# A macaron block on one core: a second norm moved to GpSimd, loads split and moved, orders of five queues rewritten

## The reference

```python
def ffn(x):                       # weights of -1, 0, 1; scales s per output
    h = silu(x @ w1.T * s1) * (x @ w2.T * s2)    # 128 -> 512
    h = gelu(h @ h1.T * sh1)                     # 512 -> 512
    h = gelu(h @ h2.T * sh2)                     # 512 -> 512
    return h @ w3.T * s3                         # 512 -> 128
def att(x):
    h = layernorm(x) * gamma + beta
    k, v = h @ Wk.T + bk, h @ Wv.T + bv
    e = exp((k @ Wka.T + bka) / sqrt(128))
    e = e / cumsum(e, axis=1)
    return cumsum(e * k, axis=1) * v
x = x + 0.5 * ffn(layernorm(x))
x = x + att(x)
x = x + 0.5 * ffn(layernorm(x))
```

## Time and profile before

| | |
|---|---|
| Median of 3 runs | 368.09 us (367.99 to 369.10) |
| The profiled execution | 368.15 us, its span 366.4 us |
| Instructions | 5194, of them 1578 products and 251 on GpSimd |
| Busy | TensorE 98%, VectorE 86%, ScalarE 77%, GpSimd 45% |
| Chain of waits | TensorE 96%, VectorE 2%, ScalarE 1%, issue 1% |
| Loads and stores | 20.94 MB, 57 GB/s on the mean |

### The profile page before, as it was taken

How to read it: one execution, slowest core, us unless ns; L and a number is a source line. 1 busy time by engine, 2 the same in 40 slices (tenths; PEclk the granted TensorE clock), 3 DMA queues, 4 the chain that set the end, 5 groups by cost and what they waited for, 6 DMA issues and landing times.

```text
span 366.4 us, 5194 instructions
## 1 busy us (share of the span) xinstructions
PE 359.3 (98%) x1578; PEld 285.1 (78%) x1578; DVE 316.2 (86%) x550; ACT 283.1 (77%) x465; POOL 163.3 (45%) x251
## 2 busy tenths in 40 slices
PE   7999999999999999999999999999999999999996
PEld 2678888787877777788778787787778777888885
DVE  5999688999989998889899989998899799857642
ACT  4998777987777879776887968877897697686763
POOL 3553344649045565812685545652573740530000
PEclk9999999999999999999999999999999999999999
DMA  7770103030100301300222012012022020040001
GB/s 245 270 294 4 54 3 107 8 110 9 58 2 0 86 29 36 83 0 2 59 59 59 1 59 59 0 59 86 0 59 88 2 86 2 4 111 2 1 30 63
DMA packets 16256, 20.94 MB, mean 57 GB/s; under 512 B 7008, under 2 KB 8288, under 8 KB 15968
## 3 DMA queue, kind: packets, MB, share of 16 engines
q1 hardware_dynamic: 15504, 19.75, 18.2%
q10 hardware_dynamic: 720, 0.80, 0.7%
HBM read 18.36 MB, written 2.18 MB: 56 GB/s over the span
## 4 chain that ended last, share of the span: by engine, by line
PE 96%; DVE 2%; issue 1%; ACT 1%; POOL 0%; POOLq 0%; ACTq 0%
PE hid_ps L643 62%; PE gate_ps L643 8%; PE y_ps L643 8%; PE up_ps L643 7%; PE y_ps L662 2%; PE xt_ps L829 2%; PE xt_ps L833 2%; PE xt_ps L836 2%; PE y_ps L843 1%; PE gate_ps L707 1%; PE up_ps L707 1%; DVE gate L1070 0%; PE xt_ps L643 0%; DVE xt_sb L1142 0%; PE xt_ps L656 0%
## 5 line engine op out<-in xcount | busy, mean ns | idle before, releaser
L643 PE MATMUL hid_ps<-act_hi,hi_h 128*128 128x512 f32 x480 | 193.3, 403 | 0.0
L643 PE MATMUL hid_ps<-act_lo,hi_h 128*128 128x512 f32 x480 | 186.7, 389 | 0.0
L1092 DVE TENSOR_TENSOR act_lo<-full,act_hi 128x512 fp32r<-128x512 f32 x185 | 132.8, 742 | 23.6 <-ACT act_hi L909 20.6
L902 ACT ACTIVATE full<-hid_ps,vec 128x512 f32<-128x512 f32 x123 | 84.1, 687 | 57.2 <-PE hid_ps L643 51.7
L643 PEld LDWEIGHTS hid_ps<-act_hi,hi_h 128*128 128x128 f32 x480 | 90.3, 188 | 22.8 <-issue 2.6
L643 PEld LDWEIGHTS hid_ps<-act_lo,hi_h 128*128 128x128 f32 x480 | 90.2, 188 | 21.3 <-issue 2.6
L909 ACT ACTIVATE act_hi<-full 128x512 fp32r<-128x512 f32 x127 | 78.6, 628 | 1.6
L567 POOL TENSOR_TENSOR xnt<-xt_sb,wide 128x512 f32<-128x512 f32 x21 | 29.4, 1400 | 45.8 <-DMA wide<-rows 45.8
L885 ACT ACTIVATE tanh<-gate_ps,s_half 128x512 f32<-128x512 f32 x60 | 40.4, 680 | 7.4 <-PE gate_ps L643 7.3
L1070 DVE SCALAR_TENSOR_TENSOR gate<-tanh,gate_ps 128x512 f32<-128x512 f32 x60 | 40.3, 674 | 6.5 <-ACT tanh L885 6.4
L1082 DVE SCALAR_TENSOR_TENSOR full<-up_ps,s_half,gate 128x512 f32<-128x512 f32 x60 | 44.1, 741 | 1.1
(11 more groups left out here) (170 smaller groups left out, 440.3 us busy)
## 6 DMA issues: line engine op xcount, KB each, us to landing
wide<-rows SPq DMA_DIRECT2D x42, 256.0 KB, 3.7
xt_sb<-xt SPq DMA_DIRECT2D x1, 2048.0 KB, 10.6
out<-xt_sb SPq DMA_DIRECT2D x7, 256.0 KB, 4.0
x_sb<-x SPq DMA_DIRECT2D x1, 1536.0 KB, 6.8
raw_h<-h2t SPq DMA_DIRECT2D x4, 256.0 KB, 7.1
raw_h<-h1t SPq DMA_DIRECT2D x2, 256.0 KB, 6.1
rows<-pair SPq DMA_DIRECT2D x21, 4.0 KB, 2.2
raw_w<-w2t ACTq DMA_DIRECT2D x1, 256.0 KB, 4.0
```

The source lines that it names most:

```text
L643: mm = eng.matmul(ps, w, a, start=(first and n == 0), stop=(last and n == len(seq_) - 1))
L902: eng.activation(full23[m % 2][:, :], home23(n, T, m)[:, :], ACT.Gelu, scale=col("sh1" if n == 2 else "sh2", m)).then_inc(s_gelu[n], 1)
L1092: eng.tensor_tensor(act_lo[a][:, m, :], full[m % 2][:, :], act_hi[a][:, m, :].bitcast(F32), ALU.subtract).then_inc(s_lo[n], 1)
```

## The change

It does these things together:

- The ones products go from 4 + 2 + 1 to 4 + 1, and the wait for the first power between them goes too.
- Tile 2 leaves `BY_PE`: its norm goes by GpSimd, the parked rows and the wide reads, as those of tiles 3 to 7. Norms aggregated on GpSimd count from 2 instead of 3.
- Act 1 of odd tiles lies in the second pair of buffers, that of even tiles in the first; before, only tile 1 used the second.
- SyncE loads x of tiles 2 and 3, and xt of tile 2, of tiles 0 and 1, and of tile 3, each by itself. x and xt of tiles 4 to 7 (1 MB each) are issued by ScalarE, just ahead of `high2.0` of tile 0.
- GpSimd's rounding of h2 and w3 becomes part of its order: h2 chunk 0 ahead of tile 2's norm, the other three and w3 behind it.
- In tile 0's first layer the half products stand in another order, flag sum 2 stands behind p1.3 in another bank (`gate_ps` instead of `y_ps`) and p1.3 no longer waits for it; `norm` of tile 0 is split into three entries.
- The orders of all five queues are written anew, the second layer of tile 0 too.

The diff, cut to its core:

```diff
-WARM_UP = (4, 2, 1)
+WARM_UP = (4, 1)
 START = {
     "PE": (
         "flag:sum1 t",
-        "p1.0 p1.1 flag:sum2 p1.2 p1.3",
+        "p1.0 p1.1 p1.2 p1.3 flag:sum2",
     ),
     "ACT": (
         "hi:w1 hi:w2 z",
-        "t vec:s1 bits:h1.1 bits:h1.3 tanh.0 tanh.1 tanh.2 high1.0 tanh.3 high1.1 z.0 z.1 high1.2 bits:h2.0 "
-        "high1.3 1:t",
+        "t vec:s1 tanh.0 bits:h1.1 bits:h1.3 bits:h2.0",
     ),
     "DVE": (
-        "stats aggr veps bits:w1 bits:w2 norm",
-        "flag:copy1 bits:h1.0 t vec:scales bits:h1.2 stats flag:raise2 aggr gate.0 veps flag:copy2 up.0 gate.1 "
-        "up.1 low1.0 gate.2 up.2 gate.3 up.3 bits:h2.1 low1.3 1:t",
+        "stats aggr veps bits:w1 bits:w2 norm.0 norm.1 norm.2 flag:copy1 0:t bits:h1.0 vec:scales bits:h1.2",
+        "gate.0 stats flag:raise2 up.0 aggr gate.1 flag:copy2 veps up.1 low1.0 gate.2 up.2 gate.3 up.3 "
+        "bits:h2.1 bits:h2.2 low1.3 1:t 2:stats flag:raise3 flag:copy3 1:gate.0 0:low2.0 1:up.0 0:low2.1 "
+        "1:gate.1 1:up.1 0:low2.2 0:low2.3 1:low1.0 1:gate.2 1:low1.1 1:gate.3 1:up.2 1:up.3",
     ),
 }
 SECOND_LAYER = (
-    "p2ahi.0 p2ahi.1 p2ahi.2 p2ahi.3 p2alo.1 p2alo.3 p2bhi.3 p2alo.0 p2alo.2 p2bhi.0 p2bhi.2 t p2blo.0 p2bhi.1 "
-    "p2blo.1 p2blo.3 p2chi.0 p2blo.2 p2clo.0 p2dhi.0 p2chi.1 p2chi.2 p2clo.1 p2dlo.0 p2chi.3 p2dhi.1 p2clo.3 "
-    "p2clo.2 p2dlo.1 flag:sum3 p1.0 p2dhi.2 p2dhi.3 p1.1 p2dlo.2 p2dlo.3"
+    "p2ahi.0 p2ahi.2 p2ahi.1 p2ahi.3 p2alo.3 p2alo.0 p2bhi.0 p2alo.2 p2alo.1 p2blo.0 p2blo.1 t p2bhi.3 "
+    "p2chi.2 p2blo.3 p2chi.0 p2chi.1 p2chi.3 p2bhi.1 p2clo.2 p2blo.2 p2dhi.2 p2clo.0 p2dhi.0 p2dlo.0 p1.0 "
+    "p2clo.1 flag:sum3 p2dhi.1 p2dlo.1 p2bhi.2 p2clo.3 p1.1 p2dlo.2 p2dhi.3 p2dlo.3"
 )
...
     "POOL": (
-        "norm",
+        "hi:h2.0 norm hi:h2.1 hi:h2.2 hi:h2.3 hi:w3 xn.0 xn.1",
         "norm xn.0 xn.1",
...
     "PE": (
-        "p1.2 p1.3 fold p3.0 p3.1",
-        "t 0:p3.2 p1.0 0:p3.3 p2.0 p1.1 p2.1 p2.2 p2.3 p4 p1.2 p1.3 a0:u p3.0 p3.1 p3.2 p3.3",
+        "p1.2 p1.3 p3.0 p3.1 p3.2 fold p3.3",
+        "p1.0 p1.1 p2.0 p2.1 p1.2 p4 p2.2 a0:u p2.3 p1.3 p3.0 p3.1 p3.2",
...
     "ACT": (
-        "bits:w3 bits:h2.3 gelu2.0 high2.0 gelu2.1 tanh.0 high2.1 tanh.1 gelu2.2 gelu2.3 high2.2 high1.0 "
-        "high2.3 high1.1 tanh.2 z gelu3.0 tanh.3 2:t high3.0 gelu3.1 high1.2 high3.1 gelu3.2 high1.3 high3.2 "
-        "gelu3.3 high3.3",
+        "0:tanh.1 0:tanh.2 0:high1.0 0:tanh.3 0:high1.1 1:z.0 1:z.1 0:high1.2 bits:w3 t 0:high1.3 bits:h2.3 "
+        "gelu2.0 tanh.0 high2.0 gelu2.1 high2.1 tanh.1 gelu2.2 gelu2.3 tanh.2 high2.2 high2.3 high1.0 high1.1 "
+        "tanh.3 gelu3.0 gelu3.1 high3.0 high3.1 high1.2 2:t high1.3 gelu3.2 high3.2 2:tanh.0 gelu3.3 high3.3",
...
     "DVE": (
-        "bits:h2.2 flag:raise3 stats low2.0 flag:copy3 aggr gate.0 veps low2.1 gate.1 up.0 up.1 low2.2 low2.3 "
-        "fold low1.0 gate.2 3:stats up.2 low1.1 2:t gate.3 up.3 low3.0 low1.2 low3.1 low1.3 low3.2 low3.3",
+        "3:stats 2:t low3.0 low3.1 low1.2 low1.3",
...
-BY_PE = (0, 1, 2)
-AGGREGATE = 3
+BY_PE = (0, 1)
+AGGREGATE = 2
...
         def first_act(T):
-            return "second" if T == 1 else 1
+            return "second" if T % 2 else 1
...
-            xload(2, NT, s_xr)
+            xload(2, 3, s_x2t)
+            eng.dma_start(xt_tile(2), xt[:, 2 * TOK:3 * TOK]).then_inc(s_xt2, 16)
+            xload(3, 4, s_x3t)
...
-            eng.dma_start(xt_sb[:, :], xt).then_inc(s_xt, 16)
+            eng.dma_start(xt_sb[:, 0:2 * TOK], xt[:, 0:2 * TOK]).then_inc(s_xt, 16)
+            eng.dma_start(xt_tile(3), xt[:, 3 * TOK:4 * TOK]).then_inc(s_xt3, 16)
...
-                    for h in range(2):
-                        for part_of, ready, first in ((xn_hi, s_xhi_half, True), (xn_lo, s_xlo_half, False)):
+                    for h, low, up in ((0, 0, 0), (0, 0, 1), (0, 1, 0), (1, 0, 0), (0, 1, 1), (1, 1, 0), (1, 0, 1), (1, 1, 1)):
...
             warm_up(WARM_UP[0])
             eng.wait_ge(s_ve, 1)
             warm_up(WARM_UP[1])
-            eng.wait_ge(s_pow, 1)
-            warm_up(WARM_UP[2])
...
             def high23(n, T, m):
+                if (n, T, m) == (2, 0, 0):
+                    eng.wait_ge(s_w3, 16)
+                    eng.dma_start(x_sb[:, 4 * TOK:], x[:, 4 * TOK:]).then_inc(s_xr, 16)
+                    eng.dma_start(xt_sb[:, 4 * TOK:], xt[:, 4 * TOK:]).then_inc(s_xtr, 16)
```

More of the change, by code:

```diff
@@ L51 @@
     "SP": (
-        "",
+        "park wide",
         "park wide",
         "a0:park a0:wide park wide",
-        "a1:park park a1:wide wide",
+        "a1:park a1:wide park wide",
         "park wide",
@@ L62 @@
         "park wide",
-        "a6:park 8:store a6:wide park wide",
-        "a7:park a7:wide 9:store park wide",
-        "10:store park 11:store wide store",
+        "a6:park a6:wide park wide",
+        "a7:park 8:store 9:store a7:wide park wide",
+        "park 10:store 11:store store wide",
         "store",
@@ L387, in items @@
                     yield stage, chunk, int(which) if which else i + AHEAD.get(stage, 0)
-        norm_of = {("ffn", t): t for t in range(2)}
-        for i, order in enumerate(STEPS["DVE"]):
+        norm_of = {}
+        for i, order in enumerate(START["DVE"] + STEPS["DVE"], -2):
             for stage, _, t in items(order, i):
@@ L428, in flag_home @@
         def flag_home(part):
-            return (hid_ps[0], y_ps, xt_ps)[part - 1][0:1, 0:1]
+            return (hid_ps[0], gate_ps[0], xt_ps)[part - 1][0:1, 0:1]
         def turn_home(n):
@@ L602, in _ @@
                     low1(stage)
-            for k in range(MC):
-                hi("h2", k)
-            hi("w3", 0)
             def emit(stage, chunk, t):
-                if stage in ("norm", "att_norm"):
+                if stage == "hi":
+                    hi(t, chunk or 0)
+                elif stage in ("norm", "att_norm"):
                     kind = "ffn" if stage == "norm" else "att"
@@ L670, in p1 @@
                         eng.wait_ge(s_whi[n], 1)
-                    for h in range(2):
-                        for part_of, ready, first in ((xn_hi, s_xhi_half, True), (xn_lo, s_xlo_half, False)):
-                            eng.wait_ge(ready, h + 1)
-                            for ps, n, done in ((gate_ps[0], "w1", s_gp), (up_ps[0], "w2", s_p1)):
-                                moved = halves(part_of, h)
-                                w, moved = (raw, moved.bitcast(F32)) if general else (whi, moved)
-                                mm = eng.matmul(halves(ps, h), wblk(w, n, 0, 0), moved, start=first, stop=not first)
-                                if not first and h == 1:
-                                    mm.then_inc(done, 1)
+                    for h, low, up in ((0, 0, 0), (0, 0, 1), (0, 1, 0), (1, 0, 0), (0, 1, 1), (1, 1, 0), (1, 0, 1), (1, 1, 1)):
+                        ready, moved = (s_xlo_half, xn_lo) if low else (s_xhi_half, xn_hi)
+                        eng.wait_ge(ready, h + 1)
+                        ps, n = (up_ps[0], "w2") if up else (gate_ps[0], "w1")
+                        moved = halves(moved, h)
+                        w, moved = (raw, moved.bitcast(F32)) if general else (whi, moved)
+                        mm = eng.matmul(halves(ps, h), wblk(w, n, 0, 0), moved, start=not low, stop=bool(low))
+                        if low and h == 1:
+                            mm.then_inc(s_p1 if up else s_gp, 1)
                     return
-                if (T, m) in ((0, 3), (1, 1)):
-                    eng.wait_ge(s_flag, T + 2)
+                if (T, m) == (1, 1):
+                    eng.wait_ge(s_flag, 3)
                 if T == 1:
@@ L1055, in norm_veps, with first_norm @@
                 eng.tensor_scalar(veps[:, :], mv[:, :, 1], 1.0, EPS, ALU.mult, ALU.add).then_inc(s_ve, 1)
[L1057 removed]
+            def first_norm(j):
                 eng.wait_ge(s_pow, 1)
[L1060 to L1062 removed]
+                eng.tensor_scalar(z[:, j * P:(j + 1) * P], norm_blk("ffn", 0, j), mv[:, j, 0:1], rstd[:, j:j + 1],
+                                  ALU.subtract, ALU.mult).then_inc(s_z, 1)
             def gate(T, m):
@@ L1117, in emit @@
                 elif stage == "norm":
-                    first_norm()
+                    first_norm(chunk)
                 elif stage == "t" and t == 0:
```

34 lines of the change are left out of this document (16 added, 18 removed), and 169 rows, old and new, of the table STEPS.

## The result

The changed kernel takes 372.85 us (median of 4 runs, 371.52 to 373.44), the kernel before beside it 368.17 (367.99 to 369.10). The ratio is 1.0117, 95% interval 1.0099 to 1.0135: slower by 1.2%, and outside the predicted range.

The account below looks back on a forecast made before the run. TensorE, busy 98% of the span, was taken to bound the kernel. From 368.15 us, gelu2.3 +0.15, turns -0.45, fold -0.07 and the wait for tile 2 +1.3 gave +0.9, so 369.0; range 367.0 to 370.2.

Parts of the forecast that it names:

- the hold: Tile 2's norm: the park waits amid ScalarE's loads, landing at 28.0, so TensorE waits 1.3 us for xn_lo.
- Turns and fold: TensorE at tile 2: four turns fewer save 0.45 us, a product's start-up saved at the fold 0.07.
- The likeliest case: Tile 2's rows are held behind ScalarE's loads: 369.0 us, between 368.4 and 369.8; chance 42%.
- rival T: Follow-up forecast for 2 KB pieces: queues alternate piece by piece, park landed near 27.5, 369 to 370 us; no chance given.
- case D: At the start, two fewer ones products let TensorE idle and delay the 2.4 GHz step: +2, 370.1 us; chance 9%.
- The start: Up to p1.3 of tile 1: first-turn gain given back, 0; gelu2.3 later behind two load issues, +0.15 us.
- the hand walk: Instruction times laid out over the first 36 us: tanh 0 at 9.35, gate 1 at 12.6, second layer from 14.1.
- ScalarE's two issues: Two loads issued ahead of high2.0 delay gelu2.3, which p1.3 waits for, by 0.15 us; bounds 0 and 0.9.
- Case C: First turn's gain is kept, tile 0's second layer starts and ends 0.5 us earlier: 366.8 us; chance 17%.

Follow-up runs that it names:

- run 1: Changed kernel with ScalarE's two 1 MB loads issued later, ahead of high3.0 instead of high2.0: 368.73 us, ratio 1.0011.
- run 9: Kernel before with ones products 4 + 1 and no wait for the first power, nothing else of the change: 368.38 us, ratio 0.9991.
- run 6: Changed kernel with ScalarE's two loads issued at the same place as four of 512 KB, in pieces of 2 KB: 371.35 us, ratio 1.0071.
- run 4: Changed kernel with five ones products put ahead of tile 2's first product to fill TensorE's pause: 371.35 us, ratio 1.0088.
- loads on SyncE (8): Changed kernel with the two 1 MB loads issued by SyncE behind xt of tile 3, instead of by ScalarE: 369.21 us, ratio 1.0030.
- run 11: The version of run 10 with ones products 4 + 1 at the start instead of 4 + 2 + 1: 367.89 us, ratio 0.9991.
- both edits (3): Changed kernel with ones products 4 + 2 + 1 again and ScalarE's loads ahead of high3.0: 368.16 us, ratio 0.9998.
- run 10: Version with both edits (3), plus three ones products behind flag sum 2 in the pause before the second layer: 367.92 us, ratio 0.9986.
- run 12: The same kernel as run 10, measured once more: 368.66 us, ratio 1.0004.
- run 2: Changed kernel with the ones products as before, 4 + 2 + 1, and the wait for the first power: 374.17 us, ratio 1.0147.
- run 7: Changed kernel with load x left ahead of high2.0 and load xt moved ahead of high3.0: 368.43 us, ratio 0.9998.
- run 5: Changed kernel with loads written for 2 KB pieces, which stayed at 8 KB, so a repeat of the changed kernel: 373.59 us, ratio 1.0131.

## Why the prediction was wrong

The start of p1.3 of tile 1 splits the 4.97 us by which the profiled span grew.

| | before | changed | predicted | measured |
|---|---|---|---|---|
| p1.3 of tile 1 starts | 25.50 | 26.76 | +0.15 | +1.26 |
| from there to the end, without the hold | 340.87 | 340.15 to 340.40 | -0.52 | -0.47 to -0.72 |
| waits for tile 2's xn_hi and xn_lo | 0 | 2.09 + 0.41 | +1.3 | +2.50 |
| clock at the 1.2 GHz level | 0 | 38.66 to 42.08 | 0 | +1.57 |
| rest | | | 0 | +0.11 to 0.36 |

The second line is the span less the start of p1.3 in the six profiles with neither a wait at tile 2 nor a fall behind it: 340.15 (run 1), 340.22 (8), 340.29 (3), 340.33, 340.37 and 340.40 (10 to 12). The fourth is the difference between profiles of the same work, with and without the fall: the thirteenth product behind the first that reads xn_lo comes 4.66 us after it in the changed kernel (38.23 to 42.89), 3.09 in its repeat (38.32 to 41.41) and 3.08 in the filled one (37.13 to 40.21). The spans agree: less p1.3's start and the two waits, the changed kernel has 371.34 - 26.76 - 2.50 = 342.08 and its repeat 369.73 - 26.58 - 2.73 = 340.42, beside the 340.15 to 340.40 of the six.

**Turns and fold: right.** The one term called a sure gain is there in all six; the two profiles of the old order have 340.87 and, run 9, 366.38 - 25.01 = 341.37. That these two differ by 0.5 with the same work bounds what such a comparison can tell.

**The hold: right in kind, too small: the term that was mis-sized.** The likeliest case put the park at 28.0 behind ScalarE's loads, because two queues took turns packet by packet. The place and the culprit hold (run 1), and so do the turns. What the working left out is that the park's pieces may come to the engines late: 3.5 to 3.6 us behind the issue in the five profiles with all of ScalarE's loads ahead of it, 0.9 to 1.0 with none or one (runs 1 and 7). With pieces of 8 KB the landing is the loads' end either way, since some ten of them an engine were left at 25.4, one microsecond behind the park's issue; with 2 KB (run 6) turns from the start would by the estimate of rival T have landed the park near 27.5, and it landed near 30.5. The term was mis-sized by the loads' end: issued at 21.68 instead of 21.1, and landed at 30.45 instead of 27.9, 8.4 us after the second issue, where 6.8 from a 1.5 MB load was used for 2 MB. With it the park landed 2.7 later than forecast (30.67), xn_lo was done at 38.2 instead of 35.8, while TensorE came 1.16 later itself: 1.3 + 2.4 - 1.16 = 2.5.

The rule of the Trainium skill, "DMA: Bandwidth & Descriptors", "Queues, rings and completion order", that an engine changes queue after some 9 to 17 descriptors, is contradicted by run 6: between 29.44 and 30.44 us one engine changed queue after every single piece.

**The clock: the step that failed outright.** The prediction weighed it only as a late rise (case D), and priced its own 1.3 us wait as 1.3 us. A pause of 2 us on TensorE may be followed by a stretch at half the clock. That puts 1.57 us more on it. By their mean clock (0.993 to 0.995) all four executions of the changed kernel have such a stretch, though only the profile says where, and the filled pause (run 4) takes 1.6 to 1.9 us off the loss.

**The start: case D's late rise, and a second mechanism.** The sum had +0.15 here. p1.3 came 1.26 late since the clock rose at 11.36: the eight half products stood 0.21 apart, tanh 0 came at 10.27 and gate 1 at 13.40. In runs with an early rise the hand walk was close: tanh 0 at 9.42, the layer at 13.93 (run 1), against 9.35 and 14.1 forecast. But the moment is different in each execution:

| profile | ones products | clock 1.00 from | low again | p1.3 starts |
|---|---|---|---|---|
| before | 4+2+1 | 6.53 | | 25.50 |
| changed | 4+1 | 11.36 | 38.66 to 42.08 | 26.76 |
| its repeat (5) | 4+1 | 5.69 | 9.11 to 12.52 | 26.58 |
| loads later (1) | 4+1 | 6.10 | | 25.51 |
| pause filled (4) | 4+1 | 6.82 | | 25.50 |
| one load early (7) | 4+1 | 6.90 | | 25.70 |
| pieces of 2 KB (6) | 4+1 | 5.53 | 8.94 to 12.35 | 27.74 |
| loads on SyncE (8) | 4+1 | 7.67 | 14.50 to 17.91 | 27.17 |
| run 11 | 4+1 | 4.98 | 8.39 to 11.81 | 26.61 |
| both edits (3) | 4+2+1 | 5.55 | | 25.42 |
| old order (9) | 4+1 | 6.62 | | 25.01 |
| run 10 | 4+2+1 | 5.17 | | 25.51 |
| run 12 | 4+2+1 | 8.00 | | 26.64 |
| run 2 | 4+2+1 | 7.67 | 38.39 to 41.80 | 26.67 |

Run 6 has the four issues in its start as well. So p1.3 starts between 25.0 and 25.7 or from 26.6 on, in the changed order with either number of ones products. With seven it was late where the rise came at 7.67 or later, behind stretched ones products. With five it was late by one late rise (11.36), and else by falls between 8 and 18 us, which D didn't have. The mean clocks of all executions, in versions where tile 2 isn't held, tell how much hangs on the ones products:

| | ones products | executions with a fall |
|---|---|---|
| kernel before | 4+2+1 | 0 of 90 |
| its order (9) | 4+1 | 1 of 12 |
| changed order (3, 10, 12) | 4+2+1 | 0 of 35 |
| changed order (1, 7, 8, 11) | 4+1 | 8 of 11, 4 of 12, 7 of 12, 2 of 11 |

The two products fewer, together with the new order, let the clock fall. By medians within a run a fall cost 1.2 us (run 1), 0.8 (run 7) and 0.9 (run 11). D's reason, the pause that the two products leave, fits this; its late rise was seen with five once, and its share in the late start of the changed kernel is not shown, since a mean clock doesn't show the moment of the rise. The table of profiles disposes of ScalarE's two issues: with them ahead of gelu2.3 (run 4) and without (run 1), p1.3 starts at 25.50 and 25.51. That term was +0.15 and is 0 for two issues; it is 1.16 for four (run 6 against run 5).

**Case C (17%)** didn't come: with the early rise too, the changed order starts p1.3 where the kernel before did. In the old order (run 9) it came 0.49 earlier with five ones products, but the span stayed the same, 366.38 against 366.37: the second layer of tile 1 still started 0.47 earlier (35.16 against 35.63), the kernel's last products only 0.2.

**What stays open.** Where the falls of the executions without a profile lay, and how often the rise comes late. What keeps the park's pieces back for 3.5 us. The 0.11 to 0.36 us that are left, and where run 9 gave back its 0.49. And why the versions without the hold, 0.5 to 0.7 us shorter behind p1.3, are not 0.15% faster in the median (0.9986 to 1.0011): falls answer it for run 1, but runs 3, 10 and 12 have none; a late start may be commoner with them, but that is argued, not shown.

## What to carry to other kernels

A load that nothing needs soon still sets the time of the small transfer issued behind it on another queue: ask what small transfer will be in flight, and put the load where none is; 4 us were won by moving two issues. A pause of TensorE of 2 us costs more than its length in some executions, so price a forecast wait with the clock behind it. Read the mean clock of every execution beside its time, not only of the profiled one: the fastest of eleven happened to be profiled in run 1 and hid what the other eight had in common. And a gain of 0.1% on one chip and ten runs may not come again: repeat the kernel itself before believing it.

## What the runs showed of the hardware

- A DMA engine that has pieces of two queues takes one of each in turn, 16 bytes and 2 KB (run 6, 29.4 to 30.4 us) as well as 16 bytes and 8 KB (changed kernel, 27.98 on), by the times of the packets. These name no engine; the clearest stretch is the one where a single engine was left.
- The pieces of a small transfer from SyncE's queue came to the engines 0.9 to 1.0 us behind its issue with none or one load of 1 MB on ScalarE's queue ahead of it (runs 1, 7), and 3.5 to 3.6 with two of 1 MB or four of 512 KB (changed kernel, runs 2, 4, 5, 6). By then most of the loads' pieces had passed. The park of tile 3 was held less by the later loads (run 10: issued 35.70, first piece 36.99, wide transfers 38.10), where TensorE didn't need it soon. Whether the making of the descriptors is what waits, no run shows.
- By the times of the pieces, one of the 16 engines finished the loads 1.2 us behind the others, with instruction packets of 0.9 and 0.3 us between its pieces. A transfer spread over 16 engines lands with the slowest.
- The granted clock rose between 4.98 and 11.36 us in the profiles of this kernel's versions, and fell to the 1.2 GHz level behind pauses (several of 0.3 to 0.5 us around the first turns, one of 1.7 or of 2.1 us later) in some executions and not in others, of one program too. A fall behind the pause at tile 2 cost 1.57 us. The Trainium skill, "TensorE: Matmul & The Clock Gate", "Part 1: The HAM clock gate (the "warmup" mystery)", says that the number of slow products at the start varies between runs of one kernel; the trace agrees.
